# Sums, differences, forward stores and the head of a spectral kernel rearranged, image reloads issued by SyncE

## The reference

```python
def _L0_conv_ref(x, w1, b1, w2, b2):
    f = jnp.fft.fft2(x, axes=(1, 2), norm='ortho')
    Xh = (f.real - f.imag)[:, :, :46, :]          # then blocks of 48 channels, 23 frequencies of W kept
    o1 = relu(einsum('bhwni,nio->bhwno', Xk, w1[0]) + b1[0])
    o2 = einsum('bhwni,nio->bhwno', o1, w2[0]) + b2[0]
    spec[:, lo:hi, :23] = softshrink(o2, 0.01)    # zero elsewhere
    return ifft2(spec, s=(H, W), axes=(1, 2), norm='ortho').real + x

def _L1_conv_ref(x, w1, b1, w2, b2):
    xf = jnp.fft.rfft2(x, axes=(1, 2), norm='ortho')   # 23 frequencies of W kept, parts xr and xi
    o1r = relu(mm(xr, w1[0]) - mm(xi, w1[1]) + b1[0])
    o1i = relu(mm(xi, w1[0]) + mm(xr, w1[1]) + b1[1])
    o2r = softshrink(mm(o1r, w2[0]) - mm(o1i, w2[1]) + b2[0], 0.01)
    o2i = softshrink(mm(o1i, w2[0]) + mm(o1r, w2[1]) + b2[1], 0.01)
    return irfft2(z, s=(H, W), axes=(1, 2), norm='ortho') + x
```

## Time and profile before

| | before |
|---|---|
| median of 3 runs | 598.96 us (593.26 to 599.08) |
| the profiled execution | 594.54 us, its span 592.6 us |
| PE busy | 479.6 us, 81% |
| DVE busy | 361.8 us, 61% |
| POOL busy | 276.7 us, 47% |
| ACT busy | 211.1 us, 36% |
| DMA | 108.29 MB, mean 183 GB/s |
| chain that ended last | PE 41%, DMA 24%, DVE 14%, POOL 10%, issue 5% |

### The profile page before, as it was taken

How to read it: one execution, slowest core, us unless ns; L and a number is a source line. 1 busy time by engine, 2 the same in 40 slices (tenths; PEclk the granted TensorE clock), 3 DMA queues, 4 the chain that set the end, 5 groups by cost and what they waited for, 6 DMA issues and landing times.

```text
span 592.6 us, 16944 instructions
## 1 busy us (share of the span) xinstructions
PE 479.6 (81%) x6944; PEld 334.2 (56%) x6944; DVE 361.8 (61%) x728; ACT 211.1 (36%) x485; POOL 276.7 (47%) x267
## 2 busy tenths in 40 slices
PE   1418789998898899798888899699997899997763
PEld 0015568776575667476566566566675666775411
DVE  6625456686576667475747656656776767666532
ACT  1203344544234433253234333254334433443101
POOL 9916542661456424671357523674258522322123
PEclk9999789999998999898997989989999999999958
DMA  8659966364897959794796938968698967633587
GB/s 179 209 115 156 210 150 169 100 176 119 226 239 150 236 144 245 210 219 136 205 256 146 243 100 207 255 151 223 168 236 206 222 188 186 165 106 100 129 222 207
DMA packets 81617, 108.29 MB, mean 183 GB/s; under 512 B 10441, under 2 KB 67903, under 8 KB 81414
## 3 DMA queue, kind: packets, MB, share of 16 engines
q1 hardware_dynamic: 64044, 61.01, 37.7%
q0 software_dynamic: 11024, 40.46, 30.0%
q10 hardware_dynamic: 6474, 5.76, 5.0%
HBM read 53.97 MB, written 53.19 MB: 181 GB/s over the span
## 4 chain that ended last, share of the span: by engine, by line
PE 41%; DMA 24%; DVE 14%; POOL 10%; issue 5%; ACT 2%; SPq 2%; POOLq 0%; DVEq 0%; ACTq 0%
DMA img<-x 20%; PE ps L718 8%; PE ps L667 6%; PE ps L705 6%; PE ps L743 6%; PE ps L624 5%; PE ps L654 5%; DVE img L595 4%; DVE uv L517 4%; POOL y L419 3%; POOL xs L397 3%; DVE ns L571 3%; SPq L327 2%; DMA jr<-scr_i 2%; ACT p L486 2%
## 5 line engine op out<-in xcount | busy, mean ns | idle before, releaser
L411 POOL TENSOR_TENSOR uv<-img 128x768 f32<-128x768 f32 (+1 forms) x48 | 101.6, 2128 | 29.9 <-DMA img<-x 29.5
L419 POOL DMA_DIRECT2D y<-img x56 | 40.1, 718 | 138.7 <-DVE img L595 134.5
L654 PE MATMUL ps<-jr,cst 64*64 64x384 f32 (+1 forms) x736 | 83.7, 518 | 13.8 <-DVE img L595 8.0
L718 PE MATMUL ps<-wt,o 128*64 128x96 f32 x1472 | 78.7, 258 | 19.7 <-DVE o L563 19.3
L667 PEld LDWEIGHTS ps<-cst,bt 128*64 128x64 f32 x1472 | 65.6, 148 | 39.1 <-issue 26.2
L718 PEld LDWEIGHTS ps<-wt,o 128*64 128x64 f32 x1472 | 69.3, 143 | 32.4 <-issue 32.4
L517 DVE TENSOR_TENSOR uv<-img 128x768 f32<-128x768 f32 (+1 forms) x48 | 63.2, 1316 | 37.7 <-DMA img<-x 35.2
L667 PE MATMUL ps<-cst,bt 128*64 128x90 f32 x1472 | 74.5, 259 | 13.8 <-DMA bt<-scr_f 13.8
L595 DVE TENSOR_TENSOR img<-ps,img 109x768 f32<-109x768 f32 x76 | 72.5, 955 | 20.9 <-PE ps L654 20.2
L397 POOL TENSOR_TENSOR xs<-xs,nt 128x360 f32<-128x360 f32 (+1 forms) x48 | 41.6, 867 | 87.3 <-DVE nt L549 66.1
L705 PE MATMUL ps<-xs,wt 64*97 64x180 f32 (+1 forms) x768 | 70.5, 321 | 12.0 <-POOL xs L397 11.7
(11 more groups left out here) (44 smaller groups left out, 456.2 us busy)
## 6 DMA issues: line engine op xcount, KB each, us to landing
y<-img POOLq DMA_DIRECT2D x28, 540.0 KB, 8.0
scr_f<-fs SPq DMA_DIRECT2D x384, 36.0 KB
scr_i<-et SPq DMA_DIRECT2D x48, 288.0 KB, 5.1
jr<-scr_i SPq DMA_DIRECT2D x92, 144.0 KB, 5.7
img<-x POOLq DMA_DIRECT2D x24, 540.0 KB, 9.9
bt<-scr_f SPq DMA_DIRECT2D x40, 288.0 KB, 6.6
y<-img POOLq DMA_DIRECT2D x14, 270.0 KB, 6.8
img<-x POOLq DMA_DIRECT2D x12, 270.0 KB, 5.4
```

What stands on the lines that cost most here:

```text
L411: nc.gpsimd.tensor_tensor(uv[n % 2][:, 1, 0:j1 - j0, :], img[t % IMGS][:, j0:j1, 0, :], img[t % IMGS][:, j0:j1, 1, :], ALU.subtract).then_ ...
L654: last = mm(ps[64 * p:64 * p + 64, B0 + a, 0:m], w_inv[c, r, :], set_rows(t, g)[c, p, 0:m], start=True, stop=True)
L718: last = mm(ps[64 * r:64 * r + 64, P2 + p, b * 2 * BS:(b + 1) * 2 * BS], o11[:, b, 2 * p + r, :], w21[:, block_no(s // STEPS, b), :], star ...
```

## The change

1. **Head.** For the first task the forward products rotate over the four bank pairs of PSUM instead of P3 alone, and the two banks of a product are copied by ScalarE and VectorE in parallel instead of both by ScalarE.
2. **Forward stores.** A group is stored in 4 transfers of 72 KB instead of 8 of 36 KB, after both copies.
3. **Reloads.** `refill` moves from GpSimd's stream to SP's. It still waits for the landing of the chunk's store; the stores of `y` stay on GpSimd. The entries of chunk 2 and chunk 3 stand earlier in the list.
4. **Order.** The inverse add gets an entry of its own, `add`. For the third inverse group of a step it stands behind `d0`. Of the two `uv` of a step, the first stands behind c1, where it stood at the end of the step before, and the second behind c0, where it stood between e and c0.

```diff
@@ schedule()
+    def both(group):
+        return [group, ("add",) + group[1:]] if group else []
...
-        first, last = inv[s][0:len(inv[s]) - 3] if len(inv[s]) > 3 else [], inv[s][max(len(inv[s]) - 3, 0):]
+        groups = [None] * (4 - max(len(inv[s]), 3)) + inv[s]
+        groups += [None] * (4 - len(groups))
         uv = [("uv",) + f[1:] for f in fwd[s]]
-        ahead = [("uv",) + f[1:] for f in fwd[s + 1]] if s + 1 < NSTEPS else []
         if s + 2 < NSTEPS:
             order.append(("load", s + 2))
         if 0 < s <= NSTEPS:
             order.append(("c1", s - 1))
-        order += first
+        order += uv[0:1]
+        order += both(groups[0])
         if s > 1:
             order.append(("e", s - 2))
-        order += uv[1:2]
-        order += last[0:1]
+        if i == 1 and t > 1:
+            order.append(("refill", t - 2, 2))
+        order += both(groups[1])
         if s < NSTEPS:
             order.append(("c0", s))
-        if 0 < s <= NSTEPS:
-            order.append(("d1", s - 1))
-        order += last[1:2]
-        if s < NSTEPS:
-            order.append(("d0", s))
+        order += uv[1:2]
         if i == 5 and t > 0:
             order.append(("refill", t - 1, 0))
         if i == 0 and t > 1:
             order.append(("refill", t - 2, 1))
+        if 0 < s <= NSTEPS:
+            order.append(("d1", s - 1))
+        order += both(groups[2])[0:1]
+        if s < NSTEPS:
+            order.append(("d0", s))
+        order += both(groups[2])[1:2]
...
         if i == 1 and t > 1:
-            order.append(("refill", t - 2, 2))
+            order.append(("refill", t - 2, 3))
...
-        order += last[2:3]
-        order += ahead[0:1]
-        if i == 1 and t > 1:
-            order.append(("refill", t - 2, 3))
+        order += both(groups[3])
@@ sync
-                    for p in range(2):
-                        sp.wait_ge(f_cp, 2 * n + p + 1)
...
+                    sp.wait_ge(*(f_cp, 2 * (n - CH + 1)) if t else (f_act, n + 1))
+                    if t == 0:
+                        sp.wait_ge(f_dve, n + 1)
+                    for a in range(2):
+                        for o in range(2):
+                            sp.dma_start(scr_f[t][o * KWP // 2:(o + 1) * KWP // 2, :, :, g, a].rearrange("k e p s c -> (k e) p (s c)"),
+                                         fs[k][64 * a + 32 * o:64 * a + 32 * o + KWP]).then_inc(f_st[k], 16)
...
+                if kind == "refill" and what[0] + IMGS < TASKS:
+                    t, c = what
+                    k, (b, f) = t % IMGS, divmod(t + IMGS, HALVES)
+                    sp.wait_ge(y_st[k][c], 32 * (t // IMGS + 1))
+                    for p in range(2):
+                        j0, j1 = jrange(*CHUNKS[c], p)
+                        sp.dma_start(folded(k, p, j0, j1), rows_of(x[b], HR * p + j0, HR * p + j1, f)).then_inc(x_ld[k][c], 16)
...
@@ scalar
+                    if t == 0:
+                        nc.scalar.activation(fs[n % FS][:, 0, :], ps[:, 2 * (g % 4), 0:2 * HC], ACT.Copy).then_inc(f_act, 1)
...
@@ vector
+                if kind == "fwd" and what[0] == 0:
+                    g = what[1]
+                    if g >= FS:
+                        dve.wait_ge(f_st[g % FS], 64 * (g // FS))
+                    dve.wait_ge(f_mm, g + 1)
+                    nc.vector.tensor_copy(fs[g % FS][:, 1, :], ps[:, 2 * (g % 4) + 1, 0:2 * HC]).then_inc(f_dve, 1)
...
@@ tensor
-                    vacate(0)
-                    vacate(1)
+                    B0 = P3 if t else 2 * (g % 4)
+                    if t > 0:
+                        vacate(0)
+                        vacate(1)
+                    elif g >= 4:
+                        pe.wait_ge(f_act, g - 3)
+                        pe.wait_ge(f_dve, g - 3)
```

49 lines of the change are left out of this document (23 added, 26 removed).

## The result

The changed kernel takes 578.01 us (median of 4 runs, 576.66 to 592.47), the kernel before 596.11 us in the same series. The ratio is 0.969 (95% interval 0.960 to 0.978): faster by 3.1% or 18 us, where 42 us were forecast. The run of 592.47 us lies in a slower state of the chip, which executions of either kernel show now and then, and the ratio leaves it out. The profiled execution took 576.66 us, 17.9 less than the 594.54 of before.

A forecast was written before the change was run, and what follows sets the result against it. Late image reloads, from full DMA engines and late issue, were taken to cost 37 us over five windows. Head 7, windows 30 and rest 2 make 39 off 594.5, 555.5, put at 557 between two scales; range 543 to 582.

The forecast's parts named there:

- engines' floor of 58.8 us per window: Six-step window without reload waits: 59.4 us, plus 0.8 for i=3, minus 1.4 for i=4 and i=5.
- The head: Before the first `a` product: 24 stores at 0.448 us each keep pace with the differences; 7 us gained, bounds 4 and 8.
- The windows: Five reload windows: 58.8 us plus 2 of waiting (bounds 0 and 7) instead of 66.8, so 30 us gained.
- SP issues chunk 0 behind the e store of step 17: Reload of chunk 0: issued about 7 us after that step's c1, so near 225 instead of 229.17.
- The rival that the reloads come no earlier: SP stands at other waits, so only head and order gain: 585.5 us, 590 on the median's scale; chance 0.05.
- i=3 row: Step with i=3: the add behind the shrinks of d0 delays the forward product; price 0.8 us, bounds 0 and 1.5.
- The weaker rival: DMA engines stay the bound, waiting moves to `jr` and `bt` loads; residual 6 us per window, 577 us; chance 0.24.
- a rest of 2: Outside the five windows: `y` stores -1.4, one i=3 step +0.8, early steps about -1.4; 2 us gained.
- The price of the queue: Reloads moved to SP's queue: 21 ns more per piece, at worst 5.3 us DMA time per window, 3.5 taken.
- The stores of `y` behind the subtraction: Steps with i=4 and i=5: c1 no longer waits for GpSimd's stores of `y`; 0.7 us gained in each.
- Slower by SP's stream: SP's wait for `y` landing blocks loads and stores behind it; at 12 us waiting per window 605 us; chance 0.05.
- the likeliest case: The forecast itself, whole kernel at 557 us, 549 to 565 by itself; chance 0.50.

## Why the prediction was right or wrong

**What bounds the kernel** was read rightly: late reloads in i=1 and i=2, with the DMA engines full from i=5 on. The engines' floor of 58.8 us per window was nearly right too: the shortest steps of the changed kernel (9.36, 9.17, 8.74, 12.40, 9.46, 10.12) make 59.3.

**The head** (term 7 us, measured 1.0) failed at "24 stores need 24 x 0.448 = 10.8 us". I carried the duration of one shape to another with twice the rows. They took 19.81 us. The rest of the sum held: with an issue of 367 ns the first `a` product stood at 33.48, against the 32.2 worked out.

**The windows** (term 30 us, measured 7.1). Of the 4.6 us by which 65.4 misses 60.8:

| steps | forecast us | measured mean us | short by |
|---|---|---|---|
| i=1 and i=2 | 17.7 + 2 | 22.4 | 2.6 |
| i=3 | 12.3 | 13.4 | 1.1 |
| i=5 (one of 13.53) | 10.2 | 10.8 | 0.6 |
| i=0 | 9.04 | 9.36 | 0.3 |
| i=4 | 9.5 | 9.5 | 0 |

The first row is the step "SP issues chunk 0 behind the e store of step 17, about 7 us after that step's c1". I looked at SP's stream and not at the wait in it: the store of chunk 0 is issued at 215.05 and landed at 226.0, so that the reload at 228.4 could come 2.4 us earlier at best, and now the store itself stands 1.1 us later. The rival that the reloads come no earlier, given 0.05, was right for chunk 0 (0.6 us earlier) and for chunks 1 and 3 (1.2 and 2.5 us later); chunk 2 came 7 us earlier, as forecast. In the i=3 row, a step forecast with 0.8 us (bounds 0 and 1.5) cost 0.9 without the fall of the clock and 2.5 with it.

By the table of the parts, the same miss reads otherwise, and worse for the sum. The waits behind the sums were 2.6 us per window, near the 2 that I left for them. What I put at nothing was what comes with them: 2.4 us for the lower clock (half of 23.9 us, over five windows, an estimate), 0.9 of stalls without a releaser and 0.7 of waiting for a `bt` load. 58.8 + 2.6 + 2.4 + 0.9 + 0.7 = 65.4. The windows of the kernel before had more time at the lower clock (30.7 us), and I had counted it all as waiting that would go.

The weaker rival, DMA engines that stay the bound with a residual of 6 us instead of 2, gave 577 us, and 578 was measured. That is luck in good part. Its residual is the 6.6 above, but it said that the waiting moves to the loads of `jr` and `bt`, and only 0.7 us did. It had a head term of 7 that was 1, and a rest of 2 that was 9.6.

**The price of the queue** (3.5 us per window) was nought. It took the packet time of q10 alone, for that of a mixed stream. In the mixed stream the engines' total is 400 us with the reloads in q1 and 401 and 412 with them in q0.

**The stores of `y` behind the subtraction** (0.7 us in i=4 and i=5) came as said, and a little more: 10.34 to 9.46 and 11.08 to 10.12. That GpSimd pays nothing for SP's wait was right: given back in the new order, it costs 44 us.

**Slower by SP's stream** did not come, but its mechanism did in part: SP's issue time grew by some 14 us per window, and one `bt` load in the five windows was waited for, 3.4 us.

The range 543 to 582 held 578; the likeliest case's own 549 to 565 didn't.

## What to carry to other kernels

Price a DMA issue by its runs, from a row of the same shape; merging stores that keep their short runs saves the issuing engine nothing, a layout that makes the runs long halves it. Before moving a load earlier, look for the landing it waits for and for what stands behind that wait on the new engine. When an edit removes a wait and the time stays, sum the idle time of the bound engine by what ended it, and its time at the lower clock, before calling the wait harmless: here 10 us of waiting went and came back as both. And an edit that measures nothing alone may be worth 14 us beside another: try the pairs before dropping it.

## What the runs showed that was not expected

- SP's issue of a 72 KB store: 762 ns with 96 runs of 768 B, 367 ns with 24 of 3072 B. Long runs did not cut the DMA engines' time: (0.531 + 0.175) x 571.7 = 404 us against 400.
- An issue on SP or ScalarE stretches from 0.33 us to over 4 while the DMA engines are full, and holds what stands behind it.
- A gap of 2.3 us before one product was followed by the lower clock level in four of six steps, which grew by 1.6 us more.
- TensorE stood up to 4.9 us in the middle of a product with no wait in the profile, and went on 1.2 to 1.8 us behind a 16 KB instruction packet. Such stalls made 0.7 us in five windows of the kernel before and up to 17 us in the others.
- GpSimd stood 9.8 us before the issue of a store, with no wait in the profile. The cause is open.
